# Attention scores in 32-query column tiles on one row half each, and a maximum pass that reads only the 160 keys a group can see

## What is computed

```
q, k, v = heads(h @ WQ + bQ), heads(h @ WK + bK), heads(h @ WV + bV)   # 16 heads of 8 features
scores = einsum('bhqd,bhkd->bhqk', q, k) / sqrt(8)
diff = i[:, None] - i[None, :]
scores = where((diff >= 0) & (diff < 128), scores, -inf)               # a causal window of 128 keys
attn = softmax(scores, axis=-1)
ao = einsum('bhqk,bhkd->bhqd', attn, v)
```

## Time and profile before

| | us |
|---|---|
| median of 3 runs | 1107.53 (1107.34 to 1107.62) |
| the profiled execution's own time | 1108.31 |
| its span, first to last instruction | 1106.5 |
| PE busy | 1005.9 (91%) |
| DVE busy | 858.5 (78%) |
| ACT busy | 671.2 (61%) |
| POOL busy | 558.8 (51%) |

### The profile page before, as it was taken

The page is one execution under the profiler, slowest core; times in us unless marked ns, Lnnn a source line. Parts: engine busy times, 40 slices in busy tenths (PEclk is TensorE's granted clock), DMA queues, the critical chain, the costliest instruction groups (busy, mean ns, idle before and its releaser), DMA issues.

```text
span 1106.5 us, 21501 instructions
## 1 busy us (share of the span) xinstructions
PE 1005.9 (91%) x7672; PEld 607.0 (55%) x7672; DVE 858.5 (78%) x2054; ACT 671.2 (61%) x998; POOL 558.8 (51%) x783
## 2 busy tenths in 40 slices
PE   3679999999999999999999999999999999999987
PEld 2234656556465565646556474655646565564635
DVE  7668887878888787898878878887888878787616
ACT  3126665657566575756657576565766666575775
POOL 6516364553736355283535537454463645535263
PEclk8689999999999999999999999999999999999999
DMA  5730514215051330605124051511405142140000
GB/s 113 171 77 1 130 35 99 65 43 102 20 118 46 85 80 7 138 21 118 46 72 85 8 135 30 114 50 58 88 20 129 35 102 62 47 89 20 19 20 10
DMA packets 86396, 74.93 MB, mean 68 GB/s; under 512 B 9426, under 2 KB 80019, under 8 KB 86291
## 3 DMA queue, kind: packets, MB, share of 16 engines
q1 hardware_dynamic: 84210, 72.78, 28.0%
q10 hardware_dynamic: 2080, 0.79, 0.3%
HBM read 36.33 MB, written 30.15 MB: 60 GB/s over the span
## 4 chain that ended last, share of the span: by engine, by line
PE 53%; DVE 23%; POOL 10%; issue 9%; ACT 2%; DMA 2%; SPq 0%; DVEq 0%; POOLq 0%; ACTq 0%
DVE mx L1017 9%; PE ps L516 8%; PE ps L498 7%; POOL h L1225 6%; PE ps L501 5%; PE ps L695 5%; PE ps L656 5%; PE ps L482 5%; PE ps L635 4%; PE ps L533 3%; PE ps L528 2%; DVE xn L874 2%; DVE junk L882 2%; POOL r L1168 2%; PE ps L550 1%
## 5 line engine op out<-in xcount | busy, mean ns | idle before, releaser
L1017 DVE TENSOR_REDUCE mx<-ps 128x2 f32<-128x512 f32 (+1 forms) x512 | 307.0, 616 | 48.9 <-PE ps L501 46.3
L772 ACT ACTIVATE pt<-ps 128x1024 f32<-128x1024 f32 (+1 forms) x256 | 232.9, 917 | 148.4 <-PE ps L482 146.5
L1178 POOL TENSOR_SCALAR_AFFINE_SELECT pt<-pt 128x512 f32<-128x512 f32 x256 | 169.3, 662 | 271.9 <-ACT pt L772 271.9
L498 PE MATMUL ps<-kd,qz 128*128 128x256 bf16 (+1 forms) x1024 | 186.4, 265 | 30.4 <-DVE mx L1017 24.6
L501 PE MATMUL ps<-mask,identb 128*128 128x512 bf16 (+1 forms) x512 | 181.8, 357 | 0.0
L498 PEld LDWEIGHTS ps<-kd,qz 128*128 128x128 bf16 x1024 | 74.3, 98 | 184.2 <-DVE mx L1017 92.2
L635 PEld LDWEIGHTS ps<-m,act_t 128*128 128x128 f32 x1024 | 127.9, 191 | 48.9 <-DVE act_t L1104 31.3
L635 PE MATMUL ps<-m,act_t 128*128 128x128 f32 x1024 | 142.1, 282 | 9.3 <-DVE act_t L1104 9.3
L516 PE MATMUL ps<-pt,va 128*32 128x256 f32 (+1 forms) x2048 | 146.2, 364 | 3.5 <-ACT ot L777 2.0
L482 PE MATMUL ps<-qz,kd 128*128 128x512 bf16 (+1 forms) x512 | 139.9, 355 | 2.2 <-DMA qz<-minus_maxima 1.2
L818 ACT ACTIVATE lin<-ps,mbias 128x512 f32<-128x512 f32 x128 | 87.8, 686 | 74.3 <-PE ps L630 40.6
(11 more groups left out here) (154 smaller groups left out, 1578.6 us busy)
## 6 DMA issues: line engine op xcount, KB each, us to landing
qz<-qk_parts SPq DMA_DIRECT2D x32, 384.0 KB
kd<-qk_parts SPq DMA_DIRECT2D x32, 384.0 KB
qk_parts<-qp SPq DMA_DIRECT2D x16, 384.0 KB, 2.4
qk_parts<-kp SPq DMA_DIRECT2D x16, 384.0 KB, 2.6
xl<-L_attn_x SPq DMA_DIRECT2D x16, 256.0 KB, 3.1
qk_parts<-qp SPq DMA_DIRECT2D x16, 256.0 KB, 2.7
qk_parts<-kp SPq DMA_DIRECT2D x16, 256.0 KB, 2.9
xnr<-xn SPq DMA_DIRECT2D x16, 256.0 KB, 2.7
```

What stands on the lines that cost most here:

```text
L498: nc.tensor.matmul(o[:, par, lo:], qz[q][:, p, par, P * i:P * (i + 1)], kd[q][:, p, P * (i - 1) + lo:P * (i + 1)], start=par == 0, stop=False,
L772: nc.scalar.activation(pt[:, n % NPT, :, 0:w_q], src, ACT.Exp, scale=SCALE).then_inc(exp_ok.sem, 1)
L1017: nc.vector.tensor_reduce(mx[:, i, h:h + 2], src, AX.X, ALU.max).then_inc(mx_ok.sem, 1)
L1178: sel1 = nc.gpsimd.affine_select(out=pt[:, s, :, 0:P], in_=pt[:, s, :, 0:P], compare_op=ALU.is_ge, fill=0.0, base=0, pattern=[[0, HG], [1, ...
```

## The change

`score_t` and `score` no longer use the whole array. Each matmul takes 32 stationary columns and the rows of one head: 51 of 64 rows for `score_t`, 48 for `score`. Four of them (c = 0 to 3) fill the 128 partitions of the output. The two row halves are used in turn: in the first half of a chunk the maximum pass works on the even heads' rows and `score_t` on the odd heads' rows, in the second half the other way round. Both are now written by one function, `scores`, and `score_t` is complete only at the end of the second half, behind `values`. A group of 32 queries reads its own 160 keys in the maximum pass, so DVE reads 2 x 160 columns instead of 2 x 256 (in the first tile of a sequence still 2 x 128), and the mask matmuls cover the two 32-wide edges (64 rows, 128 columns; in the first tile 256). `qz` has one copy, so `zrow`, its DMAs and both blankings of `qz` go; POOL builds six small masks instead of two.

```diff
-        qz = [sb(f"qz{i}", [P, NPAIR, 2, T], BF16) for i in range(2)]
+        qz = [sb(f"qz{i}", [P, NPAIR, T], BF16) for i in range(2)]
...
-            (kd[0][:].rearrange("p n t -> p (n t)").bitcast(F32), two_ones), (zrow[:], 0.0), (cp[:], 0.0),
-            (qz[0][:], 0.0), (st[:], 0.0),
+            (kd[0][:].rearrange("p n t -> p (n t)").bitcast(F32), two_ones), (cp[:], 0.0), (st[:], 0.0),
...
-                        sp.dma_start(qz[q][first + SHIFT:first + SHIFT + NPART, :, par],
-                                     zrow[:].unsqueeze(1).to_broadcast([NPART, NPAIR, T])).then_inc(stacks_in.sem, 16)
...
+            def score_t(b, q, n, par, pr):
                 g, j = n // NT, n % NT
...
+                rows = slice(64 * par, 64 * par + ROWS)
+                for c in range(NQ):
+                    mm = nc.tensor.matmul(ps[QG * c:QG * (c + 1), 2 * (n % 2) + par, 2 * P * pr:2 * P * pr + w_q],
+                                          kd[q][rows, 2 * g + pr, P * j + QG * c:P * j + QG * (c + 1)],
+                                          qz[q][rows, 2 * g + pr, P * j:P * j + w_q], start=True, stop=True)
+                return mm
+
+            def score(b, q, n, par, pr):
+                g, i = n // NT, n % NT
+                rows = slice(64 * par, 64 * par + QK)
+                w = WIN if i else P
+                for c in range(NQ):
+                    lo = P * (i - 1) + QG * c if i else 0
+                    nc.tensor.matmul(ps[QG * c:QG * (c + 1), 4 + par, w * pr:w * (pr + 1)],
+                                     qz[q][rows, 2 * g + pr, P * i + QG * c:P * i + QG * (c + 1)],
+                                     kd[q][rows, 2 * g + pr, lo:lo + w], start=pr == 0, stop=False,
+                                     skip_group_check=True)
+
+            def score_mask(n, par):
...
+                    mm = nc.tensor.matmul(o, identb[rows, 64 * par:64 * par + QG], m, start=False, stop=True, skip_group_check=True)
+                mm.then_inc(s_ps.sem, 1)
+
+            def scores(b, q, n, half):
+
+                main, nxt = has(b), has(b + 1)
+                if main and half == 0:
...
+                    if n >= 2:
+                        pe.wait_ge(*done(exp_ok, b, n - 1))
...
+                        pe.wait_ge(*done(mx_ok, b + 1, 2 * n - 1 + half))
                 for pr in range(2):
...
+                    if nxt:
+                        score(b + 1, 1 - q, n, half, pr)
+                    if main:
+                        mm = score_t(b, q, n, 1 - half, pr)
+                if main and half == 1:
+                    mm.then_inc(sT_ps.sem, 1)
+                if nxt:
+                    score_mask(n, half)
...
-                    if main and n < NCH:
-                        score_t(b, q, n)
-                    if nxt and n < NCH:
-                        score(b + 1, 1 - q, n, 0)
+                    if n < NCH:
+                        scores(b, q, n, 0)
                     if main and 3 <= n < NCH + 3:
                         values(b, q, n - 3)
-                    if nxt and n < NCH:
-                        score(b + 1, 1 - q, n, 1)
+                    if n < NCH:
+                        scores(b, q, n, 1)
...
-                            src = bank(4 + pr).rearrange("p (r k) -> p r k", r=2)[:, :, lo:]
-                            h = HG * g + 2 * pr
-                            nc.vector.tensor_reduce(mx[:, i, h:h + 2], src, AX.X, ALU.max).then_inc(mx_ok.sem, 1)
+                            src = bank(4 + pr)[:, 0:2 * w].rearrange("p (r k) -> p r k", r=2)
+                            nc.vector.tensor_reduce(mx[:, i, HG * g + pr:HG * (g + 1):2], src, AX.X, ALU.max).then_inc(mx_ok.sem, 1)
...
-                        nc.gpsimd.memset(qz[1][:], 0.0).then_inc(stacks_set.sem, 1)
```

More of the change, by code:

```diff
@@ L47 @@
 NPART = 3
-SHIFT = 6 * DH
+QK = 6 * DH
+ROWS = QK + NPART
+QG = 32
+NQ = P // QG
+WIN = P + QG
 EPS = 1e-5
@@ L90, in build @@
         identb = sb("identb", [P, P], BF16)
-        mask = sb("mask", [P, 2, 2 * P], BF16)
+        edge = sb("edge", [P, 2, 2, QG], BF16)
+        first = sb("first", [P, 2, NQ, P], BF16)
         sel = sb("sel", [P, E, P], BF16)
@@ L339, in build @@
             (half[:], -0.5), (ident[:], 0.0), (identb[:], 0.0), (bw[:, N:], 0.0), (cw[N:, :], 0.0), (ncw[:], 0.0), (b2st[:], 0.0),
-            (mask[:], 0.0), (tie[:], 0.0), (sel[:], 0.0),
+            (edge[:], 0.0), (first[:], 0.0), (tie[:], 0.0), (sel[:], 0.0),
         ]
@@ L486, in score @@
[L486 to L498, removed]
-                                     kd[q][:, p, P * (i - 1) + lo:P * (i + 1)], start=par == 0, stop=False,
-                                     skip_group_check=True)
-                nc.tensor.matmul(o[:, :, lo:], identb[:], mask[:, :, lo:], start=False, stop=True,
-                                 skip_group_check=True).then_inc(s_ps.sem, 1)
+                w_q = 2 * P if j < NT - 1 else P
@@ new lines, in score_mask @@
+            def score_mask(n, par):
+                rows = slice(64 * par, 64 * (par + 1))
+                for c in range(NQ):
+                    if n % NT:
+                        o = ps[QG * c:QG * (c + 1), 4 + par, 0:2 * WIN].rearrange("p (r e k) -> p r e k", r=2, k=QG)[:, :, 0:NQ + 1:NQ]
+                        m = edge[rows, par].unsqueeze(1).to_broadcast([64, 2, 2, QG])
+                    else:
+                        o = ps[QG * c:QG * (c + 1), 4 + par, 0:2 * P].rearrange("p (r k) -> p r k", r=2)
+                        m = first[rows, par, c].unsqueeze(1).to_broadcast([64, 2, P])
+                    mm = nc.tensor.matmul(o, identb[rows, 64 * par:64 * par + QG], m, start=False, stop=True, skip_group_check=True)
+                mm.then_inc(s_ps.sem, 1)
@@ L938, in _ @@
                 nc.vector.memset(dst, value).then_inc(blank_set.sem, 1)
-                if n == 2:
+                if n == 1:
                     norm_x(0, 0, (0, 1))
```

59 lines of the change are left out of this document (30 added, 29 removed).

## The result

| | before | after |
|---|---|---|
| median of 4 runs, us | 1107.57 (1107.34 to 1108.11) | 1155.05 (1152.58 to 1156.14) |
| mean granted clock of TensorE | 0.983 | 0.867 |
| PE / DVE / ACT / POOL busy, us | 1005.9 / 858.5 / 671.2 / 558.8 | 965.6 / 803.7 / 672.0 / 554.4 |

The account below looks back on a forecast made before the run. PE was taken to set the pace (27.17 of 28.8 us busy in a loop), DVE close behind. Profiled 1108.3 - 46 (batches 0 to 14) - 4 (first loop) + 3 (last) = 1061.3, median 0.8 lower; predicted 1060 us, range 1040 to 1118.

Parts of the forecast that it names:

- the clock falls: Rival, TensorE in the loops: small tiles count as little work, every stream doubles, over 1200 us; chance 0.02.
- issue can't keep up: Rival, PE's small matmuls: 20 pairs take 0.90 us, a chunk is 0.5 us slower, near 1290 us; chance 0.04.
- Chunks 8 to 15: Later half of each chunk loop: 7.5 and 7.15 us for 7.8 and 7.6, 0.75 less despite a new wait.
- double waits: Chunks 8 to 15: scores needs both exponential and maximum; 0.3 us added for chunks 12 to 15, 0.65 for 8 to 11.
- First eight chunks: Start of each chunk loop: 12 of DVE's 16 maxima shrink by 0.19 us each; 14.8 us becomes 12.5, 2.3 less.
- Row halves side by side: PE, half a chunk: score_t and score run at once on different row halves, 0.28 us instead of 0.55 in turn.
- Change of tiling 0.10 us: PE, between full array and quarters: 0.10 us lost each way.
- New wait for the bank-6 copy: After a head group's last chunk: values waits for ACT's copy behind a later exponential, about 1.3 us beyond PE's work.
- First loop: Maximum pass alone, before batch 0: twelve of 16 chunks save 0.35 us, four lose 0.08; 4 us less.
- Last loop: Last batch, no maximum pass: four chunks take 6.7 us instead of 5.56; 3 us more in all.

Follow-up runs that it names:

- col_late: col_early with the changed kernel's order (half of score_t in each half of a chunk, second behind values, both behind the maximum waits): 1081.8 us.
- fill_once: Changed kernel plus one burst of 512 columns of idle matmuls a chunk, in four tiles of 128 rows by 32 columns: 1116.6 us.
- row_score: narrow with the maximum pass reading one head's 48 rows instead of 128, its mask 64; score_t unchanged: 1204.4 us.
- col_early: narrow with score_t in four tiles of 32 keys on all 128 rows, same place ahead of the maximum pass: 1054.3 us, ratio 0.951.
- col_split: col_late with each half of score_t issued ahead of that half's wait for the maximum, the second still behind values: 1071.8 us.
- narrow: Kernel before with only the maximum pass changed: four tiles of 32 queries on all 128 rows, 160 keys each, DVE reading 2 x 160: 1055.73 us, ratio 0.9528.
- same_half: Changed kernel with both passes on the same row half within a half of a chunk, so they must take turns: 1259.6 us.
- row_both: Changed kernel's matmuls in the order of before: score_t on both row halves in one burst, maximum pass on 48 rows either side of values: 1093.7 us.
- pair_st: narrow with score_t in tiles of 51 rows by 32 columns, both row halves in one burst; maximum pass on 128 rows: 1053.21 us, ratio 0.9502.
- fill_tile: Changed kernel plus idle matmuls of 2 x 512 columns a chunk in four tiles of 64 rows by 32 columns: 1229.1 us.
- fill_quarter: Changed kernel plus idle matmuls of 2 x 512 columns a chunk in four tiles of 128 rows by 32 columns: 1138.9 us.
- pair_late: col_late with score_t on one row half (51 rows) in each half of a chunk, maximum pass on all 128 rows: 1181.6 us.

## Why the prediction was wrong, point by point

- **The step that failed** is the dismissal of "the clock falls" at 0.02. It rested on the earlier trace rows: the clock stayed at 1.00 at 1060 to 1071 "with half of the work in quarter tiles". Those tiles are quarters of the columns on all 128 rows. The change made tiles of 48 to 64 rows, and no row of before has those. I had said so of their concurrency and bounded that from both sides; for the clock I took the columns' row as proof. What the runs showed in its place: with few rows the clock fell to 0.50 in part of every loop. From col_late (same order, all rows) to the changed kernel it is 73 us; at least 38 of them go with the clock, since fill_once wins that much by adding work, and how the rest divides isn't shown. The rival's own price, "over 1200", was too high: the clock was low in part of the loops only. I read it so that a good part of the stretched matmuls fills time in which PE waited for DVE anyway (4.03 us busy of 6.50 at full clock); no run isolates that. The price of *issue can't keep up* was wrong in itself: 0.5 us in each of 16 chunks is 8 us a loop, not 12, and ends near 1227.
- Of the clock gate, the Trainium skill says that its ratio follows how busy PE has recently been (TensorE: Matmul & The Clock Gate, Part 1). The row disagrees if busy is the profile's busy time: 38.36 of 39.00 us at a granted clock of 0.56, and 3.96 of 4.60 us at 1.00 just before it fell (row_score).
- **Chunks 8 to 15.** I had the late `score_t` and its wait, and still forecast 7.5 and 7.15 us. At full clock col_late's transposes are 8.3 and 7.2 apart, those of col_early 7.4 and 6.5. The 0.3 and 0.65 us added for double waits were mis-sized: in col_late against col_split, waiting for maxima ahead of `score_t` costs 1.4 us a batch. (The streams of both are longer than the changed kernel's; in fill_once at full clock the stretches are 8.55 and 7.7.) I also compared the new order to before only, and so never saw that it gave away half of what the narrow maximum won. The order costs 27.5 us.
- **First eight chunks:** 13.2 us at full clock for 12.5 forecast, so 1.6 us gained instead of 2.3. DVE's maxima took 482 ns for 0.49. The chain of narrow runs through POOL's selects for about the first 10 us of its loop, so part of what DVE saves isn't collected there.
- **Row halves side by side:** right (0.02 us; same_half 1260 us).
- **Change of tiling 0.10 us:** right for full array and quarters; it also exists between 51 and 128 rows, and not between groups of tiles of 128 rows by 32 columns (in narrow, 0.06 us from a mask group of 128 columns to `values`, about its stream alone).
- **New wait for the bank-6 copy:** there, in 45 places; 36.4 / 45 = 0.8 us each, 0.5 in col_late, for 1.3 forecast.
- **First loop:** -4 forecast; the first `score_t` starts at 70.8 instead of 74.7, 3.9 less, and the loop itself, from the first `score` to the end of the last maximum, takes 18.9 us instead of 22.9, though its clock was 0.50 nearly throughout. **Last loop:** +3 forecast; the order alone makes it 4.3 us longer than col_early's (2.7 by the third transposes), and the low clock 7.6 more.
- **The sum:** narrow maximum -52, column tiles for `score_t` -1.5 (not told apart from nothing), order +27.5, few rows +73 (the clock, the changes of tiling that few rows bring and what the row halves gain, together): 47 us slower. The two last depend on each other: by way of row_both, few rows in the maximum pass cost 1093.7 - 1053.2 = 40 and the rest of the way to the changed kernel 61.

**What stays open.** Why row_score, with a longer `score_t` on all rows, lost the clock for longer than row_both. Whether the row halves would gain anything at a clock held at 1.00 in the late order was not isolated: fill_once takes 64.8 us a batch with 0.21 us of filler in each chunk, col_late 63.7. If the first burst costs the 1.5 us that the second does, 63.3 would be left, an estimate; if it costs all of its 3.4 us, 61.4. How much of the changed kernel's loss of clock comes from few rows and how much from PE's idle time behind the shorter streams wasn't isolated either: col_early and col_split show that idle time alone brings short dips. And whether it is the rows of each matmul that count, or the rows at work at one time, pair_st only hints at.

## What to carry to other kernels

When a change makes matmuls use fewer rows, price the clock first, from rows that have few rows; tiles of 32 columns on all rows are no stand-in for them, and zero rows that look like waste can be what keeps the clock up. Cut such a change into parts: here the part that helps (a narrower read by VectorE) needed neither the row tiles nor the new order. When two producers are merged into one function, look at which waits each inherits: `score_t` had no need to wait for a maximum.

## What the runs showed of the hardware that I had not expected

- The same program stretch runs at either level of the clock and can stay there for a loop: 25.5 or 39.0 us for the same 496 matmuls (row_score), 30.6 or about 43 us a loop in fill_tile. In row_score it fell after 4.6 us in which PE was busy 86%.
- Added idle matmuls on all rows made the changed kernel faster, 1155 to 1139 us (fill_quarter), and half of them to 1117; the work of fill_quarter on 64 rows made it slower, 1229.
- With tiles of 51 rows on both row halves at once the clock had only short dips in the batches and a longer one in the last loop (pair_st, 0.963, against 0.967 of col_early); one half at a time, in the other order, it fell to 0.903 (pair_late).
